# Two of eight experts of the second layer computed for every token, in the middle of the threshold search

## The chip, the cores and the metric

One core of one Trainium2 chip. The metric is the device time of one execution in microseconds (us). Three runs of the kernel before gave 168.7, 170.29 and 170.41 us.

## The reference

1024 tokens of 128 channels, in float32, go through two layers, each a conditioning step and a mixture of eight experts of width 512.

```python
x = x + L0_ffn(L0_cond(x, cond_8, ...), ...)     # each token takes its 2 best experts
x = x + L1_ffn(L1_cond(x, cond_8, ...), ...)     # each expert takes its 256 best tokens

# L1_ffn, the part that the change is about (n = 1024, k = 256, e = 8)
S = sigmoid(xt @ Wg).T                  # 8 x 1024 scores
G, I = top_k(S, k)                      # per expert: its 256 tokens and their scores
ex = xt[I]
hid = gelu(einsum('ekh,ehf->ekf', ex, W1) + b1[:, None, :])
out = (einsum('ekf,efh->ekh', hid, W2) + b2[:, None, :]) * G[..., None]
new_x = zeros_like(xt).at[I.reshape(-1)].add(out.reshape(-1, h))
```

## The kernel before

Each engine's program is written out by hand in one block, in the order in which the engine runs it; semaphores tie the engines together. TensorE keeps its order strictly: what stands behind a waiting instruction waits too. Tokens lie in eight chunks of 128 (`NC`), and `P` is 128.

The first layer ends with `x1`, which from there on is the running sum for the output. The second layer's conditioning (`turn_x1`, `up_gate`, `down1`, `turn_d`) gives each chunk's result twice: transposed in `dT` (channels on the partitions, all 1024 tokens side by side), and by token in `row`, which together with the scores goes to DRAM as `rows1`.

Then each expert's 256th highest score is searched (L1050 to L1075). VectorE compares all 1024 scores of an expert with 16 candidate thresholds at once (L1060), decides which hold at least 256 tokens (L1061), and TensorE adds those decisions up with one small matmul (L624 for the first digit, L628 for the five others), which gives the next digit of `tau`. After six digits TensorE spreads `tau` (L631), VectorE marks the tokens above and at it, TensorE counts the marks ahead of each token (L489 to L642), and VectorE turns the counts into slots, `hlf1h` and `loc1` (L1091 to L1099). ScalarE and GpSimd each make one half of `hlfv` from them (L825, L431).

Per expert, `place` on VectorE (L1103) and `find_slots` on TensorE (L649, eight small matmuls) give the list of tokens, `index` (L875) stores it as integers, and GpSimd issues two indirect gathers of 128 rows each (L420). `turn_xg` transposes the rows (L658), ScalarE copies them into `xgT` (L833, `take_xg`), `up1` makes 256 of the 512 hidden columns (L669, in halves h = 0 and 1), ScalarE applies the gelu (L842, two instructions for each half), and `down_e` makes the results (L679) for 128 tokens at a time. VectorE adds the bias (L1123) and multiplies with the score (L1125), `score`.

How the results get back to the tokens differs. Experts 0 to 5: GpSimd scatters them into a zeroed DRAM plane of the expert (`add`, L427, two instructions), SyncE loads the plane back (L322) once both have landed (`added`), and VectorE adds the plane to the running sum, 128x1024 at a time (`take_part`, L1132). Experts 6 and 7: VectorE builds a one-hot matrix from the token list (`spread_rows`, L1116), and TensorE multiplies the results with it, which spreads them over all tokens (`spread_out`, L689); VectorE adds that from PSUM (L1153).

GpSimd's queue is: gathers of experts 0 to 4, then for each expert its two scatters and the gathers of the expert five ahead. ScalarE's order in the expert loop is `take_xg(e + 1)`, then the gelus of expert e; TensorE's is `turn_xg(e + 1)`, `up1(e, 0)`, `down_e(e - 1)`, `up1(e, 1)`. `keep_warm` (L450) are matmuls on ones whose result nobody reads.

## Time and profile before

| | |
|---|---|
| median of three runs | 170.29 us (168.7 to 170.41) |
| profiled execution, its own time | 169.11 us |
| its span, first to last instruction | 167.3 us |
| mean granted TensorE clock | 0.939 |
| PE busy | 141.0 us (84%) |
| PE weight loads (PEld) busy | 117.8 us (70%) |
| DVE (VectorE) busy | 92.5 us (55%) |
| ACT (ScalarE) busy | 72.8 us (44%) |
| POOL (GpSimd) busy | 64.4 us (38%) |

The profiled execution's time is its span and 1.8 us around it. Busy shares are averages over stages of very different kinds; the conditioning of layer two ends at about 96 us, the threshold search at about 108 us, and the experts' matmuls at 163.65 us. A granted clock of 1.00 is TensorE at 2.4 GHz, of 0.50 at 1.2 GHz.

### The profile page before, as it was taken

Reading aid. Unit: us, or ns where it says so; the run is one execution under the profiler, and the core shown is the slowest. Engines: PE = TensorE matmul, PEld = TensorE weight load, DVE = VectorE, ACT = ScalarE, POOL = GpSimd, SP = SyncE. Lnnn points to the kernel's source line nnn. Section 1 sums busy time; section 2 is a strip of 40 time slices with the busy share of each in tenths; the row PEclk is TensorE's granted clock in tenths of the full one; section 3 lists DMA queues with packets and bytes.
Section 4 is the critical chain, followed back from the end, with each engine's and each line's share of the span. In section 5 each row is a group of like instructions: output and inputs, shape, how many; then the busy total and the mean of one; then the engine's idle time right before and its main releaser. Section 6 shows DMA issues by size and latency. Waiting matters only on the chain.

```text
span 167.3 us, 3393 instructions
## 1 busy us (share of the span) xinstructions
PE 141.0 (84%) x1044; PEld 117.8 (70%) x1044; DVE 92.5 (55%) x302; ACT 72.8 (44%) x223; POOL 64.4 (38%) x67
## 2 busy tenths in 40 slices
PE   7998959999999999994999720188889988899991
PEld 3756439999988999743999610045479877788990
DVE  0489391565553554415767988764353368436182
ACT  1678325777765656301478540000145444434100
POOL 0000376544476445624000000015777777776000
PEclk9999996999999999999699995559999999999999
DMA  5999827998898921127069240000122345515804
GB/s 163 355 427 345 254 67 218 325 297 277 281 299 246 313 108 47 35 64 220 0 264 402 92 133 0 0 2 21 50 50 66 93 135 173 174 52 157 233 17 125
DMA packets 20419, 27.52 MB, mean 164 GB/s; under 512 B 2034, under 2 KB 14706, under 8 KB 20146
## 3 DMA queue, kind: packets, MB, share of 16 engines
q1 hardware_dynamic: 17410, 22.78, 41.2%
q0 software_dynamic: 1920, 4.00, 8.0%
q10 hardware_dynamic: 1072, 0.52, 1.1%
q8 instruction: 9, 0.15, 0.4%
q14 instruction: 8, 0.07, 0.1%
HBM read 20.71 MB, written 6.59 MB: 163 GB/s over the span
## 4 chain that ended last, share of the span: by engine, by line
PE 55%; DMA 14%; DVE 12%; POOL 9%; issue 6%; ACT 1%; DVEq 0%; ACTq 0%; POOLq 0%
PE bank L538 10%; PE bank L548 9%; PE bank L679 6%; PE bank L580 5%; PE bank L689 4%; PE bank L669 4%; DMA xs<-rows,gidx 4%; DVE bsc L1060 4%; DMA xg<-rows,idx 4%; POOL xg L420 3%; DMA rows<-c_tok 2%; POOL plane L427 2%; PE bank L450 2%; DMA got<-picked 2%; PE bank L589 2%
## 5 line engine op out<-in xcount | busy, mean ns | idle before, releaser
L763 ACT ACTIVATE hT<-bank,w_now 128x128 f32<-128x128 f32 x92 | 26.2, 368 | 13.6 <-PE bank L538 13.6
L394 POOL DMA_INDIRECT xs<-rows,gidx x16 | 15.5, 969 | 27.7 <-DMA rows<-c_tok 18.8
L538 PE MATMUL bank<-xg,w_now 128*128 (+1 forms) x184 | 25.5, 283 | 0.0
L548 PE MATMUL bank<-w_sb,hT 128*128 (+1 forms) x184 | 25.1, 281 | 0.3 <-ACT hT L763 0.3
L548 PEld LDWEIGHTS bank<-w_sb,hT 128*128 128x128 f32 x184 | 23.2, 198 | 0.5 <-ACT hT L763 0.5
L538 PEld LDWEIGHTS bank<-xg,w_now 128*128 128x128 f32 x184 | 23.2, 198 | 0.5 <-issue 0.5
L450 PE MATMUL bank<-ones 128*128 128x512 bf16 x81 | 22.0, 418 | 1.1 <-DVE ones L877 1.1
L842 ACT ACTIVATE h1T<-bank,c_sb 128x256 f32<-128x256 f32 x32 | 13.4, 470 | 19.0 <-PE bank L669 19.0
L399 POOL DMA_INDIRECT picked<-y,sidx x16 | 15.4, 962 | 13.3 <-DVE y L982 12.1
L420 POOL DMA_INDIRECT xg<-rows,idx x16 | 16.9, 1058 | 6.3 <-issue 4.0
L669 PE MATMUL bank<-xgT,v_sb 128*128 128x256 f32 x64 | 16.5, 383 | 0.5 <-ACT xgT L833 0.5
L976 DVE TENSOR_TENSOR yt<-bank,b_sb 128x128 f32<-128x128 f32 x23 | 6.7, 291 | 18.0 <-PE bank L548 15.8
L679 PEld LDWEIGHTS bank<-v_sb,h1T 128*128 128x128 f32 x128 | 15.3, 192 | 1.0 <-ACT h1T L842 0.8
L679 PE MATMUL bank<-v_sb,h1T 128*128 128x128 f32 x128 | 15.9, 277 | 0.1
L427 POOL DMA_INDIRECT plane<-x_sb,idx x12 | 13.6, 1136 | 3.7 <-issue 2.7
L450 PEld LDWEIGHTS bank<-ones 128*128 128x128 bf16 x81 | 8.2, 109 | 9.4 <-issue 2.2
L431 POOL TENSOR_TENSOR hlfv<-hlf1h,cst 128x128 bf16<-128x128 bf16 x1 | 0.8, 776 | 34.5 <-DVE hlf1h L1099 34.5
L1123 DVE TENSOR_TENSOR yb<-bank,c2b_sb 128x128 f32<-128x128 f32 x16 | 4.7, 291 | 15.4 <-issue 9.3
L669 PEld LDWEIGHTS bank<-xgT,v_sb 128*128 128x128 f32 x64 | 11.0, 191 | 1.6 <-ACT xgT L833 0.7
L951 DVE COPY w_now<-w_sb 128x516 f32 (+1 forms) x23 | 11.0, 477 | 1.5 <-issue 1.5
L982 DVE SCALAR_TENSOR_TENSOR y<-yt,pairm,y 128x128 f32 (+1 forms) x23 | 8.1, 351 | 5.6 <-DVE yt L976 5.5
L580 PE MATMUL bank<-x1T,cw_sb 128*128 128x128 f32 x64 | 9.6, 298 | 0.0
(183 smaller groups left out, 208.0 us busy)
## 6 DMA issues: line engine op xcount, KB each, us to landing
v_sb<-in_v SPq DMA_DIRECT2D x16, 256.0 KB
cw_sb<-in_cond_w SPq DMA_DIRECT2D x8, 386.5 KB
plane<-y SPq DMA_DIRECT2D x6, 512.0 KB, 4.7
w_sb<-plane SPq DMA_DIRECT2D x6, 512.0 KB, 4.2
w_sb<-in_w SPq DMA_DIRECT2D x1, 2064.0 KB, 9.1
w_sb<-in_w SPq DMA_DIRECT2D x1, 1536.0 KB, 12.3
rows<-row SPq DMA_DIRECT2D x1, 544.0 KB, 3.4
xT_sb<-in_xT SPq DMA_DIRECT2D x1, 512.0 KB, 3.8
```

Source lines behind the costliest of these rows:

```text
L394: pool.indirect_dma_start(out=xs[:, b % RING], out_offset=None, in_=rows0, in_offset=rows_at(gidx, b)).then_inc(gathered[b % RING], 16)
L399: pool.indirect_dma_start(out=picked, out_offset=rows_at(sidx, b), in_=y0[:, b], in_offset=None).then_inc(scattered, 16)
L420: pool.indirect_dma_start(out=xg[:, i], out_offset=None, in_=rows1, in_offset=rows_at(idx1, i)).then_inc(gathered1[e], 16)
L427: pool.indirect_dma_start(out=plane[e], out_offset=rows_at(idx1, i), in_=y1[:, e % Y1_RING, h], in_offset=None).then_inc(added[e], 16)
L450: pe.matmul(out_bank[:], ones[:], ones[:].unsqueeze(1).to_broadcast([P, 4, P]), start=True, stop=True)
L538: mm = pe.matmul(bank[2 + j % 2][:, P * f:P * f + P], w1_now[:, j % WB_RING, P * f:P * f + P], xsT[:, bass.ds((j - e) * P, P)], start=True ...
L548: mm = pe.matmul(bank[6 + j % 2][:, 0:C], hT[:, j % 2, P * f:P * f + P], w2_sb[:, bass.ds(e * (NF * C) + f * C, C)], start=(f == 0), stop= ...
L580: mm = pe.matmul(bank[2 + b % 2][:, P * m:P * m + P], cw_sb[:, b, P * m:P * m + P], x1T[:, b % 2], start=True, stop=True)
L669: mm = pe.matmul(bank[2 + u % 3][:, CAP * f:CAP * f + CAP], v1_sb[:, e, P * fc:P * fc + P], xgT[:, e % 2], start=True, stop=True)
L679: mm = pe.matmul(bank[6 + h][:, 0:C], h1T[:, e % 2, f, P * h:P * h + P], v2_sb[:, e, f], start=(f == 0), stop=(f == NF - 1))
L763: ins = act.activation(hT[:, j % 2, P * f:P * f + P], bank[2 + j % 2][:, P * f:P * f + P], ACT.Relu, bias=w1_now[:, j % WB_RING, F + f:F + ...
L842: act.activation(h1T[:, e % 2, fc], bank[2 + (2 * e + h) % 3][:, CAP * f:CAP * f + CAP], ACT.Gelu, bias=c1_sb[:, e * NF + fc:e * NF + fc + ...
```

## The change

Experts 6 and 7 are no longer routed. They are computed for all 1024 tokens, straight from `dT`, as eight units of 256 tokens; a unit has the same matmuls and gelus as a routed expert. Six of these units (expert 6 whole and half of expert 7) stand in TensorE's order between the steps of the threshold search, the counts and the `find_slots`; the two others come at the very end. The count's PSUM moves to banks 0 and 1, the up projections use four banks (`UP_BANKS`), and the down projections two, then three (`y_bank`).

ScalarE copies the results of the six early units out of PSUM (`take_yd`), after the table load for the gelu. VectorE weights them with `wd`, which is the score where the token is among the expert's 256 and 0 elsewhere, and adds them to the running sum (`take_dense`: a bias add over up to 128x1024, then one multiply-add of 128x128 for each chunk). The results of the last two units are added straight from the bias add (`add_dense`).

`spread_rows`, `spread_out`, L1153 and GpSimd's iota go, as do two of the eight `find_slots`, `index` and gather pairs, and all `keep_warm` in this part. The six routed experts run as units 6 to 11. In ScalarE's new order `take_xg(e)` stands behind both gelus of the unit before it. VectorE makes the half of `hlfv` that ScalarE made. The plane of expert 5 is added before the last unit's results.

The diff, cut to its core:

```diff
-PLANES = 6
+SPARSE = 6
+DENSE = E - SPARSE
...
+        yd = w2_sb[:, 2 * T:4 * T].rearrange("p (e c d) -> p e c d", e=DENSE, c=NC)
+        wd = sb("wd", [P, NC, DENSE])
...
+        CHUNKS = T // CAP
+        HEAD = 6
+        UNITS = DENSE * CHUNKS + SPARSE
+        unit = [(True, SPARSE + d // CHUNKS, d % CHUNKS) for d in range(DENSE * CHUNKS)]
+        unit[HEAD:HEAD] = [(False, e, 0) for e in range(SPARSE)]
+        TAIL = range(HEAD + SPARSE, UNITS)
+        UP_BANKS = (4, 5, 2, 3)
+
+        def y_bank(n, h):
+            return 6 + n % 2 if n < HEAD else (6, 7, 1)[(NH * (n - HEAD) + h) % 3]
...
-            pool.iota(iota_t, [[1, T]], base=0, channel_multiplier=0,
-                      allow_small_or_imprecise_dtypes=True).then_inc(iota_ready, 1)
...
-                if e + GATHERS_AHEAD < E:
+                if e + GATHERS_AHEAD < SPARSE:
...
+            def count_experts(s):
                 pe.wait_ge(enough_ready, s + 1)
-                pe.matmul(bank[4][:, 0:1], same[:], enough[:], start=True, stop=True).then_inc(counted, 1)
-
-            pe.wait_ge(tau_ready, 1)
-            pe.transpose(bank[5][:, 0:P], tau[:].to_broadcast([P, P]), ident).then_inc(tau_spread, 1)
-
-
-            pe.wait_ge(gteq_ready, 1)
-            running_counts(bank[2][:, 0:NC * E], gteq[:, 0], E)
-
-            for d in range(NC):
-                pe.matmul(bank[3][:, 0:NC * E], ones[:], gteq[:, 0, d * E:(d + 1) * E].unsqueeze(1).to_broadcast([P, NC, E]),
-                          start=(d == 0), stop=False)
-            for d in range(1, NC):
-                pe.matmul(bank[3][:, d * E:NC * E], ones[:], gteq[:, 1, 0:(NC - d) * E], start=False, stop=False)
-            pe.matmul(bank[3][:, 0:NC * E], tri[:], gteq[:, 1], start=False, stop=True).then_inc(prefix1, 1)
+                if s == 0:
+                    for i in range(2):
+                        mm = pe.matmul(bank[1][:, 0:1], same[:], coarse_enough[:, i:i + 1], start=(i == 0), stop=(i == 1))
+                else:
+                    mm = pe.matmul(bank[1][:, 0:1], same[:], enough[:], start=True, stop=True)
+                mm.then_inc(counted, 1)
...
+            def up1(n, h):
+                dense, e, q = unit[n]
+                rows_in = dT[:, CAP * q:CAP * q + CAP] if dense else xgT[:, e % 2]
+                if not dense:
+                    pe.wait_ge(xgT_ready, e + 1)
+                u = 2 * n + h
+                if u in (2, 3):
+                    pe.wait_ge(sc_ready, u - 1)
+                if u >= 4:
+                    pe.wait_ge(h1T_ready, 2 * (u - 4) + 2)
                 for f in range(2):
                     fc = 2 * h + f
-                    mm = pe.matmul(bank[2 + u % 3][:, CAP * f:CAP * f + CAP], v1_sb[:, e, P * fc:P * fc + P],
-                                   xgT[:, e % 2], start=True, stop=True)
+                    mm = pe.matmul(bank[UP_BANKS[u % 4]][:, CAP * f:CAP * f + CAP], v1_sb[:, e, P * fc:P * fc + P],
+                                   rows_in, start=True, stop=True)
                 mm.then_inc(h1_ready, 1)
 
-            def down_e(e):
-                pe.wait_ge(h1T_ready, 4 * (e + 1))
+            def down_e(n, h):
+                dense, e, q = unit[n]
+                pe.wait_ge(h1T_ready, 4 * (n + 1))
+                if n == 0:
+                    pe.wait_ge(row_ready, NC)
+                if 2 <= n < HEAD:
+                    pe.wait_ge(yd_kept, n - 1)
+                if n == HEAD:
+                    pe.wait_ge(yd_kept, HEAD)
+                    pe.wait_ge(idx1_ready, SPARSE)
+                if NH * (n - HEAD) + h >= 3:
+                    pe.wait_ge(y1_ready, NH * (n - HEAD) + h - 2)
+                for f in range(NF):
+                    mm = pe.matmul(bank[y_bank(n, h)][:, C * h:C * h + C], h1T[:, n % 2, f, P * h:P * h + P],
+                                   v2_sb[:, e, f], start=(f == 0), stop=(f == NF - 1))
+                mm.then_inc(y1_sent, 1)
+
+            pe.wait_ge(in_v, 16 * 2 * E)
...
+            up1(0, 0)
+            turn_scores(0)
+            count_experts(0)
+            up1(0, 1)
+            turn_scores(1)
+            count_experts(1)
+            up1(1, 0)
+            down_e(0, 0)
+            down_e(0, 1)
+            count_experts(2)
+            up1(1, 1)
+            up1(2, 0)
+            down_e(1, 0)
+            count_experts(3)
+            down_e(1, 1)
+            up1(2, 1)
+            up1(3, 0)
+            count_experts(4)
+            down_e(2, 0)
+            down_e(2, 1)
+            up1(3, 1)
+            count_experts(5)
+            up1(4, 0)
+            spread_tau()
+            down_e(3, 0)
+            count_ahead()
+            down_e(3, 1)
+            up1(4, 1)
+            up1(5, 0)
+            find_slots(0)
+            down_e(4, 0)
+            find_slots(1)
+            down_e(4, 1)
+            find_slots(2)
+            up1(5, 1)
+            find_slots(3)
+            down_e(5, 0)
+            find_slots(4)
+            down_e(5, 1)
+            find_slots(5)
+            turn_xg(0)
+            up1(HEAD, 0)
+            turn_xg(1)
+            up1(HEAD, 1)
+            for n in range(HEAD + 1, UNITS):
+                e = n - HEAD
+                if e + 1 < SPARSE:
+                    turn_xg(e + 1)
+                up1(n, 0)
                 for h in range(NH):
+                    down_e(n - 1, h)
+                up1(n, 1)
+            for h in range(NH):
+                down_e(UNITS - 1, h)
...
-            act.wait_ge(hlf1h_ready, 1)
-            act.activation(hlfv[:, :, :, 0].rearrange("p c e h -> p (c e) h"), hlf1h[:], ACT.Identity,
-                           scale=const("pcol")).then_inc(hlfv_ready[0], 1)
...
+            def take_yd(n):
+                _, e, q = unit[n]
+                act.wait_ge(y1_sent, NH * n + NH)
+                act.activation(yd[:, e - SPARSE, NH * q:NH * q + NH], bank[6 + n % 2][:, 0:NH * C], ACT.Copy).then_inc(yd_kept, 1)
+
+            for n in range(UNITS):
+                gelu(n, 0)
+                if 1 <= n <= HEAD:
+                    take_yd(n - 1)
+                e = n - HEAD + 1
+                gelu(n, 1)
+                if 0 <= e < SPARSE:
+                    take_xg(e)
...
+            v.wait_ge(hlf1h_ready, 1)
+            v.tensor_scalar(hlfv[:, :, :, 0].rearrange("p c e h -> p (c e) h"), hlf1h[:], const("pcol"), None,
+                            ALU.mult).then_inc(hlfv_ready[0], 1)
...
+            def add_dense(d, c, src):
+                return v.scalar_tensor_tensor(x1[:, c], src, wd[:, c, d:d + 1], x1[:, c], ALU.mult, ALU.add)
+
+            def take_dense(d, chunks):
+                c0, c1_ = NH * chunks[0], NH * chunks[-1] + NH
+                v.wait_ge(yd_kept, CHUNKS * d + chunks[-1] + 1)
+                now = yd[:, d, c0:c1_]
+                link(v.tensor_tensor(now, now, bc(c2b_sb[:, SPARSE + d], 1, c1_ - c0), ALU.add))
+                for c in range(c0, c1_):
+                    ins = add_dense(d, c, yd[:, d, c])
+                link(ins)
+
...
+            link(v.scalar_tensor_tensor(wd[:], posi[:].rearrange("p (c e) -> p c e", e=E)[:, :, SPARSE:E], float(CAP),
+                                        sc[:, :, SPARSE:E], ALU.is_lt, ALU.mult))
+            for d in range(HEAD // CHUNKS):
+                take_dense(d, range(CHUNKS))
+            if HEAD % CHUNKS:
+                take_dense(HEAD // CHUNKS, range(HEAD % CHUNKS))
+            for e in range(SPARSE):
                 for h in range(NH):
                     score(e, h)
-                if e == 0:
-                    index(E - 1)
-                if e == 2:
-                    spread_rows()
                 if e >= 3:
                     take_part(e - 3)
-            for e in range(E - 3, PLANES):
+            for e in range(SPARSE - 3, SPARSE - 1):
                 take_part(e)
-            for g in range(2):
-                v.wait_ge(summed, g + 1)
-                v.tensor_tensor(acc[:, 512 * g:512 * g + 512], acc[:, 512 * g:512 * g + 512], bank[(1, 5)[g]][:],
-                                ALU.add).then_inc(out_ready, 1)
+            for n in TAIL:
+                _, e, q = unit[n]
+                if n == TAIL[-1]:
+                    v.wait_ge(part_in[SPARSE - 1], 16)
+                    for g in range(2):
+                        ins = v.tensor_tensor(acc[:, 512 * g:512 * g + 512], acc[:, 512 * g:512 * g + 512],
+                                              part[SPARSE - 1][:, 512 * g:512 * g + 512], ALU.add)
+                        if g == 0:
+                            ins.then_inc(out_ready, 1)
+                        else:
+                            link(ins)
+                for h in range(NH):
+                    with_bias(n, h)
+                    ins = add_dense(e - SPARSE, NH * q + h, yb[:, n % 2, h])
+                if n < TAIL[-1]:
+                    link(ins)
+            ins.then_inc(out_ready, 1)
```

## Rows read from the trace of the kernel before

**Rows 1.** Windows: stretch; length, busy PE, PEld, DVE, ACT, POOL; granted clock; DMA share, GB/s

```profile
96.00:109.34 13.34, 2.33 (x15) 1.25 (x13) 10.52 (x42) 2.15 (x7) 0.00 (x0) 0.64 0.14 42
```

**Rows 2.** Chain that ended last, two turns of the search: start, length, what

```profile
101.67 0.20 PE bank L628
...
103.75 0.20 PE bank L628
```

**Rows 3.** Timeline of PE and ACT as conditioning ends: start, length, engine, line

```profile
95.62 1.12 PE L618 MATMUL bank<-cst,got 128*128 128x128 f32 x8
...
97.08 1.28 ACT L823 ACT_TABLE_LOAD   x1
```

**Rows 4.** Chain that ended last, from the counts to the first gathers

```profile
109.34 0.23 PE bank L489
...
110.43 0.09 PE bank L642
...
112.33 0.79 POOL hlfv L431
...
114.83 1.02 POOL xg L420
...
116.16 2.91 DMA xg<-rows,idx
...
121.15 0.43 PE bank L649 x8
```

**Rows 5.** Timeline, first routed expert and a later gather issue

```profile
119.58 0.38 ACT L833 ACTIVATE xgT<-bank 128x256 f32<-128x256 f32 x1 [6.90 <-PE bank L658]
...
121.19 0.84 ACT L842 ACTIVATE h1T<-bank,c_sb 128x256 f32<-128x256 f32 x2 [1.22 <-PE bank L669]
...
121.56 0.94 POOL L420 DMA_INDIRECT xg<-rows,idx  x1 [0.30 <-issue]
```

**Rows 6.** Chain that ended last, pieces of the expert loop and its end

```profile
127.36 0.22 PE bank L658 x2
...
147.95 1.78 PE bank L679 x16
149.74 0.88 PE bank L669 x4
...
154.51 3.57 PE bank L689 x32
...
163.67 0.69 DVE c_tok L1153
```

**Rows 7.** Timeline of VectorE and GpSimd, scatters and a plane's addition

```profile
139.84 0.99 POOL L427 DMA_INDIRECT plane<-x_sb,idx  x1 [0.30 <-issue]
...
150.10 0.29 DVE L1125 TENSOR_SCALAR x_sb<-yb,xg 128x128 f32<-128x128 f32 x1
...
150.30 1.22 DVE L1132 TENSOR_TENSOR c_tok<-c_tok,w_sb 128x1024 f32<-128x1024 f32 x1
150.38 1.97 POOL L427 DMA_INDIRECT plane<-x_sb,idx  x1 [0.31 <-DVE x_sb L1125]
```

**Rows 8.** Loads of the planes, by tile: one stretch's instruction and its landing

```profile
L322 SPq DMA_DIRECT2D w_sb<-plane x1: 360/360/360, 142.1 to 142.1; - x1
...
DMA to landing us min/median/max: 4.1/4.1/4.1
```

**Rows 9.** Loads of the planes, the last two together

```profile
L322 SPq DMA_DIRECT2D w_sb<-plane x2: 360/360/360, 153.4 to 154.9; - x2
...
DMA to landing us min/median/max: 4.0/4.8/5.5
```

**Rows 10.** Line L399, layer one's scatters: ns min/median/max, first and last start

```profile
L399 POOL DMA_INDIRECT picked<-y,sidx x16: 957/957/983, 43.5 to 71.4; - x16
```

**Rows 11.** Windows as in Rows 1, around a fall and a rise of the clock

```profile
79.50:80.00 0.50, 0.50 (x4) 0.50 (x4) 0.10 (x1) 0.26 (x1) 0.00 (x0) 0.50 0.00 0
...
82.50:83.00 0.50, 0.50 (x5) 0.50 (x5) 0.50 (x3) 0.48 (x2) 0.00 (x0) 0.76 0.00 0
```

More of the change, by code:

```diff
@@ L694, in _ @@
-            pe.wait_ge(in_v, 16 * 2 * E)
-            keep_warm(bank[7], 6)
-            for hlfv_part in hlfv_ready:
-                pe.wait_ge(hlfv_part, 1)
-            for e in range(AHEAD):
-                find_slots(e)
-                keep_warm(bank[7], 3)
-            turn_xg(0)
-            up1(0, 0)
-            find_slots(AHEAD)
-            up1(0, 1)
-            find_slots(AHEAD + 1)
-            turn_xg(1)
-            find_slots(AHEAD + 2)
-            down_e(0)
-            up1(1, 0)
```

144 lines of the change are left out of this document (50 added, 94 removed).

## The prediction

> **What bounds the kernel now.** I read the granted clock first, then the chain of waits, then the timeline from 95 us to the end, engine by engine. During the threshold search VectorE alone is busy: between 96 and 109.34 us it works 10.5 of 13.3 us and TensorE 2.3, at a mean clock of 0.64 [rows 1]. One digit takes 2.08 us from one counting matmul to the next [rows 2]. That idle time is what the change wants to fill. Behind the search the chain goes over counts, slots and the first gather [rows 4], and from about 120 us to 163.65 us TensorE is the bound almost without a break, the last pieces being the spreads of experts 6 and 7 [rows 6]. The planes of experts 0 to 5 come back beside that. The last load starts at 154.9 and lands between 158.9 and 160.4 us (4.0 or 5.5 later [rows 9]), which VectorE can still take before the last spread. I therefore ask of the change how late the experts' phase starts, how fast TensorE gets through it, and what then comes last.
>
> **TensorE's work.** A half of `up1` costs 0.87 us and the two halves of `down_e` 1.78 [rows 6], so a unit is 2 x 0.87 + 1.78 = 3.52 us. Before there are eight units (28.2 us) and 64 spread matmuls in two pieces, 7.6 us (the first piece shows 3.57 for 32 records [rows 6], and there are 64 of them). After there are 14 units, 49.3 us, of which six (21.1) lie in the head. In the experts' phase eight units stay, as before, and the spreads go. If nothing else stood in the way, that would be the gain: 7.6 us less what the head takes longer.
>
> **The head.** I take 95.6 us, where TensorE begins the score transposes now [rows 3], and add what it must do up to the end of `up1(6, 1)`: six units 21.1, the two halves of unit 6 1.7, transposes 1.1 [rows 3], six digit matmuls of 0.20 [rows 2] 1.2, the spread of `tau` 0.3 (an estimate; it is one transpose), counts 1.1 (109.34 to 110.52 [rows 4], at 1.2 GHz; at 2.4 GHz down to 0.6), six `find_slots` between 0.43 [rows 4] and 0.65, taken at 0.5, 3.0, and two transposes of gathered rows with the first copy 1.0 [rows 5, 6]. That is 30.5 us. To it come gaps. The first two digit decisions come from VectorE as before, and TensorE stands some 0.5 us before each. The larger gap is a new wait: `down_e(0, 0)` needs four gelus, and ScalarE must first copy the scores (0.4), load its table (1.28 [rows 3]) and do two pairs of 0.84 [rows 5]. With the second transposes done at 99.0 that is 102.5 us, while TensorE has finished `up1(1, 0)` at 100.6: 1.9 us of waiting, and `count_experts(2)` is queued behind it, so the search stands still too. With 0.3 for switching, `up1(6, 1)` ends at 95.6 + 30.5 + 1.0 + 1.9 + 0.3 = 129.3 us.
>
> In the search itself each digit leaves TensorE about 1.9 us before the next decision, and the list puts 2.6 to 3.5 us of unit work between them (three or four halves). The count is late each time, and VectorE waits. Following the list item by item, the third count falls at 104.3 instead of 101.67 [rows 2], `tau` is spread near 113.7, the counts end at 115.8 instead of 110.5, `hlfv` is there at about 118.4 (2.6 us for the slots and `hlfv` as now, 110.52 to 113.12 [rows 4]), and the first gather starts at 120.1 instead of 114.83 [rows 4]. It lands 4.2 us later (two issues and 2.91 [rows 4]), before TensorE wants it at 126.6. The delay of the search by 5 us is thus covered by unit work; the cover is thin only where units are done and slots are not. The `hlfv` half that moves from ScalarE to VectorE, and `wd`, are single small instructions of about 0.25 us each (estimate; every small VectorE instruction here takes 0.15 to 0.3): at most 0.3 us on the path, inside the rounding. The iota and the cleared `keep_warm` cost nothing and free nothing that anyone waits for.
>
> **The routed phase has a new stall.** Before, ScalarE copied `xgT` of the next expert ahead of both gelus of this one. Now `take_xg(e)` stands behind `gelu(n, 1)`, and that gelu needs `up1(n, 1)`, the last item of the turn. TensorE's next item, `turn_xg(e + 1)`, overwrites the PSUM that this copy reads, and waits for it. Whatever was gathered early, TensorE stands each turn for two gelus (0.84), a copy (0.38) and two handovers of 0.04 [rows 5]: 1.27 us. This happens ahead of `turn_xg(2)` to `turn_xg(5)` and once more ahead of `up1(11, 0)`, five times, 6.3 us. Nothing in the trace of before shows this wait, as the order was another; its bounds are 0 (were the copy free to go first) and 1.3 us each, and I take the upper one, because every part has its row and the order admits no other. The five turns are 4 x (1.27 + 0.27 + 3.52) + (1.27 + 3.52) = 25.0 us, and the first half of the sixth, `up1(12, 0)` and `down_e(11)`, 2.65. `down_e(11, 1)` ends at 129.3 + 25.0 + 2.7 = 157.0 us.
>
> VectorE and GpSimd keep up with this. `take_dense` is one bias add of 1.22 (as L1132 [rows 7]) and eight multiply-adds, about 4 us, and for the two chunks of expert 7 another 2; it ends near 133 us and makes the first `score` 1.6 us late. GpSimd then scatters expert 0 and gathers expert 5 by 139, landing by 143.5 at the latest (behind a plane load of 4.1 to 5.5 us [rows 8, 9]). TensorE wants it at 145.8, thanks to the stalls.
>
> **The end.** Between `down_e(11, 1)` and TensorE's last matmul lie three halves of `up1` and two pairs of `down_e`, 6.2 us: until 163.2. That is no later than 163.65 now, so TensorE's end, two VectorE steps (1.0) and the 2.94 us from VectorE's last instruction to the end of the span (163.67 + 0.69 to 167.3 [rows 6]) would give 167.1. But the plane of expert 5 now has only these 6.2 us to come back. The result is scored 0.65 us after its matmul (149.74 to 150.39 [rows 6, 7]), at 157.65. The second scatter starts 0.6 us later, behind the first (0.99 and 0.3 each [rows 5, 7]), and as `take_part(2)` has just started on VectorE it loses about 0.55 more: a scatter that started 0.08 us into a plane's addition took 1.97 instead of 0.99 [rows 7]. From an undisturbed start to the plane's arrival it is 6.4 us (139.84 to 142.1 and 4.1 [rows 7, 8]), at most 7.8 (5.5 in place of 4.1 [rows 8, 9]); I take the first, since no second load runs beside it. The plane is in at 157.65 + 0.6 + 0.55 + 6.4 = 165.2. Then come two additions of 128x512 (1.3, half of 1.22 each and a handover [rows 7]), two bias adds and two multiply-adds of 128x128 (four of some 0.33, 1.35), and 2.94 to the end. 165.2 + 1.3 + 1.35 + 2.94 = 170.8 us of span, against 167.3: 3.5 us more, 2.1%. The profiled execution's time lies 1.8 us above its span, which makes 172.6 against 169.1. The median of the runs before is 1.2 us above that execution; on it I forecast 170.3 + 3.5 = 173.8 us.
>
> **A rule that speaks against this.** The scatters in layer one, which run beside VectorE's multiply-adds with both inputs in SBUF (L982), take 0.957 to 0.983 us [rows 10], so those short instructions hold nothing up; only the 1.22 us addition does. The Trainium skill, GPSIMD Engine Reference, section "Key points", says that GpSimd shares its SBUF interfaces with VectorE and contends with instructions that have two SBUF inputs. By that rule taken strictly all of `take_dense` would hold up the gathers, which is what rival 3 prices; the trace agrees for the long form only.
>
> **Rivals.** (1) A clock fall in the head. After the pause between the layers the clock was at 0.50 by 79.5 us and rose between 82.5 and 83.0 [rows 11], so some 3.3 us at 1.2 GHz. The 0.5 and 1.9 us gaps could bring that on, and TensorE, now the bound of the head, would lose half of it: +1.7, 175.5 us. Against it speaks that work resumes at once. (2) The plane is not last. If its way back, from score to landing, took 3.7 us less than the 7.5 that I reckon, TensorE's end would decide: 167.1 of span, 170.1 us, no change. No load in the rows is that fast. (3) Gathers held up by `take_dense`: 6 us of it instead of 1, expert 5 lands at 147 instead of 143.5, TensorE waits 1.5 us: 175.3. (4) The other side: no stall for `xgT`, because ScalarE's copy gets done in time. The point is whether `take_xg` ends before `up1(n, 1)` does. Then 6.3 us go, the gather of expert 5 becomes the wait (2 us), the chain over the plane stays: span 166.5, 169.5 us. Were the plane hidden as well, it would be span 162.8 (without the gather's wait 160.8), 165.8 us: faster. Whether the digits come somewhat earlier or later changes none of this, as unit work fills the head either way.
>
> **How the numbers follow.** Forecast 173.8, chance 0.40. Rival 1 0.20, rival 3 0.08, rival 2 0.15, rival 4 with the plane last 0.09, with both wrong 0.08. About 1% is what a measurement of this kernel can tell from no change, that is 168.6 to 172.0 us. Faster is the last case, 0.08. Same are rival 2, rival 4's first form and the lower edge of the forecast (the head 1.5 us shorter), 0.27. Slower is the rest, 0.65. The range goes from 169.3, just under the cases of no change, to 176.3 us, the clock's case with 0.8 for the bounds of the plane's way and the counts.
>
> **What the profile would show.** Right: a granted clock near 1.00 in place of 0.64 during the search; digits 2.5 to 4 us apart; one TensorE gap near 101 us for L842's gelu; the first `find_slots` about 5 us later; then five gaps of 1.3 us ahead of the transposes, released by ScalarE's copy; and at the end VectorE waiting for a DMA, some 2 to 4 us after TensorE's last matmul. Wrong, if those five gaps are missing or are released by gathers, if the last plane arrives before TensorE ends, or if the clock falls to 0.50 between 100 and 130 us.

## The result and the profile after

The changed kernel takes 176.19 us (median of four runs, 175.26 to 177.23) against 169.5 us for the kernel before (four runs, 168.63 to 170.41). The medians lie 6.7 us apart (4.0%). The ratio on record is 1.0465 with a 95% interval of 1.0419 to 1.0512, which would be some 7.8 us; the eight times do not account for the difference, and this text goes by the medians and the trace. Slower it is by either. The forecast was slower by 3.5 us (2.1%). Medians here are of all executions, while ratios leave out those more than 1.5% above the same kernel's fastest. The profiled execution took 175.26 us, its span 173.3 us.

The page of the changed kernel first: busy time by engine, and TensorE's granted clock in 40 slices of 4.3 us.

```profile
PE 147.7 (85%) x1086; PEld 125.3 (72%) x1086; DVE 92.3 (53%) x308; ACT 83.5 (48%) x250; POOL 58.2 (34%) x62
...
PEclk9999999999999999999999969999999999999998
```

The clock stands near full speed through the search, where it was 0.64 [rows 1]; one slice, from 99.6 us, shows a 6. The timeline of TensorE, by its own waits, through the threshold search (start, length, instruction, and in brackets the idle time before it and what ended it):

```profile
95.31 0.20 PE L633 MATMUL bank<-coarse_enough,same 128*128 128x1 bf16 x2 [0.40 <-DVE coarse_enough L1088]
...
97.42 0.18 PE L635 MATMUL bank<-enough,same 128*128 128x1 bf16 x1 [0.50 <-DVE enough L1093]
...
100.27 3.65 PE L703 MATMUL bank<-v_sb,h1T 128*128 128x128 f32 x16 [1.70 <-ACT h1T L873]
...
103.75 0.17 PE L635 MATMUL bank<-enough,same 128*128 128x1 bf16 x1
...
109.55 0.17 PE L635 MATMUL bank<-enough,same 128*128 128x1 bf16 x1
...
112.59 0.17 PE L635 MATMUL bank<-enough,same 128*128 128x1 bf16 x1
...
124.12 1.16 PE L703 MATMUL bank<-v_sb,h1T 128*128 128x128 f32 x8 [0.45 <-ACT h1T L873]
```

The first two digits are 2.1 us apart, as before [rows 2]. Then TensorE stands 1.70 us ahead of `down_e(0, 0)`, with the third count queued behind it (6.3 us to the next digit), and from there the digits are 2.7 to 3.1 us apart, because unit work lies in front of each. The `down_e(0)` that follows takes 3.65 us for 16 matmuls, where the same pair behind the same pause takes 2.05 in the runs below whose clock stays up: the clock has fallen. In the pause itself (98.60 to 100.20 us) it was still granted at 1.00. The windows around it (length, busy PE, PEld, DVE, ACT, POOL, then the granted clock), and those of the two stages:

```profile
95.30:130.20 34.90, 31.35 (x236) 26.99 (x236) 18.80 (x62) 14.80 (x37) 8.34 (x9) 0.95 0.10 29
130.20:159.30 29.10, 22.29 (x150) 19.52 (x150) 11.27 (x33) 11.55 (x30) 15.36 (x15) 1.00 0.37 110
...
101.00:102.00 1.00, 1.00 (x7) 1.00 (x6) 0.00 (x0) 0.00 (x0) 0.00 (x0) 0.50 0.00 0
103.00:104.00 1.00, 1.00 (x7) 0.99 (x7) 0.00 (x0) 0.04 (x1) 0.00 (x0) 0.68 0.00 0
```

In the head TensorE works 31.35 of 34.9 us; in the routed rounds only 22.29 of 29.1. Where most of those 6.8 us go is seen at the transposes of the gathered rows, again on TensorE's timeline:

```profile
131.56 0.41 PE L671 MATMUL bank<-cst,xg 128*128 128x128 f32 x2 [1.35 <-ACT xgT L864]
...
136.84 0.41 PE L671 MATMUL bank<-cst,xg 128*128 128x128 f32 x2 [1.35 <-ACT xgT L864]
...
142.12 0.41 PE L671 MATMUL bank<-cst,xg 128*128 128x128 f32 x2 [1.35 <-ACT xgT L864]
...
147.40 0.41 PE L671 MATMUL bank<-cst,xg 128*128 128x128 f32 x2 [1.36 <-ACT xgT L864]
...
152.59 1.13 PE L686 MATMUL bank<-xgT,v_sb 128*128 128x256 f32 x4 [1.26 <-ACT xgT L864]
```

Five gaps, each released by ScalarE's copy (line 864, which was line 833), 5.28 us from one turn to the next. The end of the span, from the chain of waits:

```profile
159.54 0.96 POOL plane L434
...
160.81 3.12 DMA plane<-x_sb,idx
...
163.94 3.92 DMA w_sb<-plane
...
167.95 0.10 DVE c_tok L1201
...
170.19 0.35 DVE c_tok L1167
```

The last result of expert 5 is scattered, its plane is loaded, and only then can VectorE finish. TensorE has ended at about 167.2 us (163.65 before); the load lands at 167.86.

To compare kernels I use the **stage** from the first digit matmul (line 624 before, 633 after) to the end of the span. What lies ahead of it is nearly the same work in every kernel here and still ended between 95.3 and 100.3 us in the traces of the chips without the unexplained waits shown further below. Before it is 97.47 to 167.3, 69.8 us; after it is 95.31 to 173.3, 78.0 us, of which 1.6 us is the clock (3.65 against the 2.05 us that the same 16 matmuls take in the traces where the clock stays up), so 76.4 without. The changed kernel's digit is 2.2 us earlier in part because its clock did not fall between the layers, where the kernel before spent 3.3 us near half speed [rows 11]. So of the fall one pays about as much in either trace, and 76.4 - 69.8 = 6.6 us agrees with the medians' 6.7. A stage is read from one execution each.

### The profile page after: what moved, and what is told of

It reads as the page before. It is cut to its first block, busy times and chain, and to the rows that moved or that the text cites. A ratio compares the mean times of both kernels' runs of the same rounds, so it can differ in the third digit from the quotient of the medians.

```text
span 173.3 us, 3525 instructions
## 1 busy us (share of the span) xinstructions
PE 147.7 (85%) x1086; PEld 125.3 (72%) x1086; DVE 92.3 (53%) x308; ACT 83.5 (48%) x250; POOL 58.2 (34%) x62
## 4 chain that ended last, share of the span: by engine, by line
PE 59%; DMA 14%; ACT 8%; DVE 8%; issue 5%; POOL 3%; ACTq 0%; DVEq 0%; POOLq 0%
PE bank L703 13%; PE bank L545 10%; PE bank L686 9%; PE bank L555 9%; ACT h1T L873 5%; DMA xs<-rows,gidx 4%; PE bank L587 3%; DMA w_sb<-plane 2%; PE bank L457 2%; DMA got<-picked 2%; DMA rows<-c_tok 2%; DMA plane<-x_sb,idx 2%; POOL picked L408 2%; PE bank L662 2%; PE bank L596 1%
## 5 line engine op out<-in xcount | busy, mean ns | idle before, releaser
L873 ACT ACTIVATE h1T<-bank,c_sb 128x256 f32<-128x256 f32 x56 | 23.3, 472 | 25.8 <-PE bank L686 25.5
L703 PE MATMUL bank<-v_sb,h1T 128*128 128x128 f32 x224 | 30.6, 290 | 3.6 <-ACT h1T L873 3.1
L703 PEld LDWEIGHTS bank<-v_sb,h1T 128*128 128x128 f32 x224 | 28.5, 202 | 6.5 <-ACT h1T L873 6.2
L403 POOL DMA_INDIRECT xs<-rows,gidx x16 | 15.7, 980 | 26.2 <-DMA rows<-c_tok 17.9
L434 POOL DMA_INDIRECT plane<-x_sb,idx x12 | 12.7, 1055 | 13.1 <-DVE x_sb L1157 10.9
L457 PE MATMUL bank<-ones 128*128 128x512 bf16 x63 | 16.1, 406 | 1.1 <-DVE ones L909 1.1
L686 PE MATMUL bank<-w_eff,v_sb 128*128 128x256 f32 x64 | 16.1, 386 | 0.0
L427 POOL DMA_INDIRECT xg<-rows,idx x12 | 12.9, 1074 | 5.7 <-issue 3.0
L686 PE MATMUL bank<-xgT,v_sb 128*128 128x256 f32 x48 | 12.6, 384 | 1.7 <-ACT xgT L864 1.7
L686 PEld LDWEIGHTS bank<-w_eff,v_sb 128*128 128x128 f32 x64 | 11.4, 191 | 1.2
L457 PEld LDWEIGHTS bank<-ones 128*128 128x128 bf16 x63 | 6.5, 106 | 7.9 <-issue 1.1
```

The costliest lines, as they stand in the source:

```text
L403: pool.indirect_dma_start(out=xs[:, b % RING], out_offset=None, in_=rows0, in_offset=rows_at(gidx, b)).then_inc(gathered[b % RING], 16)
L427: pool.indirect_dma_start(out=xg[:, i], out_offset=None, in_=rows1, in_offset=rows_at(idx1, i)).then_inc(gathered1[e], 16)
L434: pool.indirect_dma_start(out=plane[e], out_offset=rows_at(idx1, i), in_=y1[:, e % Y1_RING, h], in_offset=None).then_inc(added[e], 16)
L457: pe.matmul(out_bank[:], ones[:], ones[:].unsqueeze(1).to_broadcast([P, 4, P]), start=True, stop=True)
L686: mm = pe.matmul(bank[UP_BANKS[u % 4]][:, CAP * f:CAP * f + CAP], v1_sb[:, e, P * fc:P * fc + P], rows_in, start=True, stop=True)
L703: mm = pe.matmul(bank[y_bank(n, h)][:, C * h:C * h + C], h1T[:, n % 2, f, P * h:P * h + P], v2_sb[:, e, f], start=(f == 0), stop=(f == NF ...
```

## The experiments

Four questions: does the place of `take_xg` make the five gaps; does the pause ahead of `down_e(0, 0)` bring the clock down; is the plane last at the end; and is the late search really covered by unit work?

**The copy ahead of the gelu.** In ScalarE's loop:

```
                 e = n - HEAD + 1
+                if 1 <= e < SPARSE:
+                    take_xg(e)
                 gelu(n, 1)
-                if 0 <= e < SPARSE:
+                if e == 0:
                     take_xg(e)
```

> The changed kernel, with one line of ScalarE's order moved: take_xg(e) stands between the two gelus of a unit instead of behind both (for experts 1 to 5). Theory A (the order makes the five pauses of 1.35 to 1.7 us ahead of the transposes of gathered rows): the pauses go or shrink below 0.3 us, save one wait of up to 2 us for the gather of expert 5; the rounds fall from 5.28 us towards 3.9 us and the time falls by 4 to 6.5 us against the changed kernel, to 170 to 172 us. Rival B (the rounds are paced by GpSimd's queue and the planes, and the copy only happens to be the releaser): the pauses stay, released by a DMA, and the time falls by less than 2 us.

Measured: 171.17 us, 1.0149 of before (1.0036 to 1.0261; before 168.91 on that chip), so it is 2.3 us slower than the kernel before beside it where the change was 6.7: some 4.4 us of the 6.7 are gone (5.3 by the two ratios). The stage is 72.1 us, 4.3 less than 76.4. Its timeline of TensorE at the same transposes:

```profile
130.32 0.41 PE L671 MATMUL bank<-cst,xg 128*128 128x128 f32 x2 [0.54 <-ACT xgT L864]
134.09 0.38 PE L671 MATMUL bank<-cst,xg 128*128 128x128 f32 x2
137.99 0.38 PE L671 MATMUL bank<-cst,xg 128*128 128x128 f32 x2
142.60 0.44 PE L671 MATMUL bank<-cst,xg 128*128 128x128 f32 x2 [0.54 <-DMA xg<-rows,idx]
```

and its chain of waits:

```profile
138.07 4.49 DMA xg<-rows,idx
...
153.63 0.96 POOL plane L434
...
154.90 4.29 DMA plane<-x_sb,idx
...
159.20 4.02 DMA w_sb<-plane
```

A turn takes 3.8 to 3.9 us in place of 5.28 and its gap is gone (0.54 us of the first one stay): the copy's place was the cause. Not all of the five gaps' 6.7 us came back, for two reasons that these rows show. The gather of expert 5, which the gaps had given time, is now waited for (142.60 comes 4.6 us after the turn before). And the plane's way back is longer: its scatter's data take 4.29 us where they took 3.12, so that from the end of `down_e(11)`'s first half to the end of the span it is 16.0 us (152.62 to 168.6) against 14.8 (158.53 to 173.3).

**The table load ahead of the scores.** `act.activation(scrap[:], bb_sb, ACT.Gelu)`, which loads the table of gelu, moved ahead of the loop that copies the scores:

```
+            act.activation(scrap[:], bb_sb, ACT.Gelu)
             for g in range(2):
                 act.wait_ge(s_turned, g + 1)
 ...
-            act.activation(scrap[:], bb_sb, ACT.Gelu)
```

> The changed kernel, with the gelu's table loaded ahead of the two score copies, where ScalarE waits for TensorE anyway, instead of behind them. Theory A (the pause ahead of down_e(0, 0) costs its own 1.7 us and brings a stretch at 1.2 GHz, which costs about 1.8 us more): the pause falls below 0.5 us, the clock stays at 1.00 through the search, and the time falls by 3 to 3.5 us. Rival B (the clock's fall has nothing to do with the pause): 1.2 to 1.6 us less, and the clock still falls. Rival C (the head has slack before the gathers): less than 1 us.

Measured: 174.51 us, 1.0382 (1.029 to 1.0475); stage 74.75, 1.65 less than 76.4. Its rows of the first digit, of `down_e(0)` and of the first transposes:

```profile
97.35 0.20 PE L633 MATMUL bank<-coarse_enough,same 128*128 128x1 bf16 x2 [0.39 <-DVE coarse_enough L1088]
...
100.79 2.05 PE L703 MATMUL bank<-v_sb,h1T 128*128 128x128 f32 x16 [0.18 <-ACT h1T L873]
...
126.02 0.41 PE L671 MATMUL bank<-cst,xg 128*128 128x128 f32 x2
```

The pause of 1.70 us is 0.18, and the stage is shorter by about that much. The load cost what the pause showed and nothing more. Of the expectations the size is rival B's, but the clock stays up behind the pause, as theory A had it. The last row, the first transposes of gathered rows, is used further below.

**The pause filled.** `down_e(0, 0)` still waits as long, but TensorE does idle matmuls in the meantime:

```
             up1(1, 0)
+            keep_warm(bank[7], 7)
             down_e(0, 0)
```

> The changed kernel, with seven matmuls on ones that nobody reads put into TensorE's pause ahead of down_e(0, 0); the pause itself stays, filled. Theory A (the pause is what lets the clock fall): the two halves of down_e(0) take 1.8 us instead of 3.65, and the time falls by 1.6 to 2 us. Rival B (the clock falls at some time of its own in any case): no change of the time beyond 0.8 us, and a stretch at 0.50 elsewhere in the head.

Measured: 176.69 us, 1.0437 (1.033 to 1.0543); stage 76.5. No gain, which is rival B's size. Its timeline:

```profile
101.32 1.67 PE L457 MATMUL bank<-ones 128*128 128x512 bf16 x7
103.18 2.05 PE L703 MATMUL bank<-v_sb,h1T 128*128 128x128 f32 x16 [0.19 <-ACT h1T L874]
```

The clock stays up behind the filled pause. But it also stayed up behind the unfilled one, in the run with the copy moved (101.46) and in the next one (105.21):

```profile
101.46 2.05 PE L703 MATMUL bank<-v_sb,h1T 128*128 128x128 f32 x16 [1.70 <-ACT h1T L873]
```
```profile
105.21 2.05 PE L703 MATMUL bank<-v_sb,h1T 128*128 128x128 f32 x16 [1.69 <-ACT h1T L873]
```

So a fall can follow this pause and need not, and the filled run does not show that the filling prevented one. Both of these unfilled runs had a fall between the layers (slices of 8 and 7 near 80 us), and so had the filled one (0.50 between 80 and 82 us). The run of the changed kernel had none there and one here. One later run (six early units refitted, below), in which the pause is 0.18 us, had none in either place. Why a run takes one or the other is not settled.

**Without the last plane.** This kernel leaves out the wait for the plane of expert 5 and adds the plane of expert 4 a second time in its place, so its output is not the right one; the instructions stay the same.

```
-                    v.wait_ge(part_in[SPARSE - 1], 16)
 ...
-                              part[SPARSE - 1][:, 512 * g:512 * g + 512], ALU.add)
+                              part[SPARSE - 2][:, 512 * g:512 * g + 512], ALU.add)
```

> The changed kernel without its last wait: the plane of expert 5 is not added at the end, plane 4 is added there a second time in its place, so that the instructions are the same and only the wait for the load of plane 5 goes. It shows what the plane's way back costs at the end. Theory A (the plane is last, by what the trace shows: it lands 0.6 us after TensorE's last matmul and two additions follow): the time falls by 2 to 2.7 us. Rival B (TensorE's end would set the time anyway, with the additions behind it): less than 1 us.

Measured: 174.87 us, 1.0352 (1.0249 to 1.0456); stage 74.65, 1.75 less (it begins late in this trace, at 100.25 us, which the stage's length leaves out). The chain now passes over the plane of expert 4:

```profile
160.23 2.56 DMA plane<-x_sb,idx
...
162.80 4.09 DMA w_sb<-plane
```

The last plane costs 1.75 us at the end, as much as VectorE's wait for it in the changed kernel (1.80 us ahead of line 1201) and a little less than the 2 to 2.7 us of theory A. Rival B's less than 1 us is out.

**Both edits together, and other sizes of the head.** The next kernels all take the copy and the table edit (the first has only these), and the others write TensorE's list anew so that only as much unit work stands between two digits as fits into the time VectorE takes, with 6, 5 or 4 of the eight dense units ahead of the routed ones (`HEAD`); the rest come last:

```
+up1(0, 0) turn_scores(0) count_experts(0) up1(0, 1) turn_scores(1) count_experts(1)
+up1(1, 0) down_e(0, 0) count_experts(2) down_e(0, 1) up1(1, 1) count_experts(3)
+up1(2, 0) down_e(1, 0) count_experts(4) down_e(1, 1) up1(2, 1) count_experts(5)
+spread_tau() count_ahead() up1(3, 0) down_e(2, 0) down_e(2, 1) find_slots(0)
+up1(3, 1) find_slots(1) down_e(3, 0) find_slots(2) down_e(3, 1) find_slots(3)
+up1(4, 0) find_slots(4) up1(4, 1) find_slots(5)
+down_e(4, 0) down_e(4, 1)
```

This is the list for five units. For four, only `find_slots(4)` and `find_slots(5)` stand behind `find_slots(3)`; for six, `up1(5, 0)` stands ahead of `down_e(4, 0)` and the rest of unit 5 at the end.

> Both edits of the first two experiments together: take_xg between the gelus, the gelu's table loaded early. From the first digit's matmul (L633) to the end of the span the changed kernel takes 76.4 us where its clock does not fall, the kernel before 69.8; the first edit gave 72.1, the second 74.75. Theory A (the two add up, since one shortens the head and the other the rounds): 70.6 us of this stage, and a time within 1% of the kernel before. Rival B (the plane of expert 5 or the gathers take back what the head gives): 71.5 us or more.

> As e5, still six early units, but in another order on TensorE: never more than two halves (1.8 us) between two digits, none between the last digit and the counts, three ahead of the first find_slots, and the other ten between and behind the find_slots. The digits thus keep their 2.1 us. Theory A (the prediction's: unit work fills TensorE in the head whichever way it is ordered, so late digits cost nothing): within 0.7 us of e5's stage. Rival B (the delayed digits delay slots, gathers and everything behind them): 2 us or more faster than e5.

> As e6, with five early units and three at the end. Theory A (about four units fit into TensorE's idle time in the search; each further one lengthens the head by 2 to 3.5 us and the end loses 3.5, but the plane of expert 5 then waits at the end): the three at the end, 9.8 us of TensorE behind the last routed result, just cover the plane's 7.7 us and the additions, so the stage takes 65 to 67.5 us, and the time is 1.5 to 3% below the kernel before. Rival B (gathers and GpSimd's queue pace the rounds): 69 us or more, no gain on the kernel before.

> As e6, with four early units (expert 6) and four at the end (expert 7): the early work is what fits into the search without delaying it. Theory A: the first find_slots starts 15.7 to 16.5 us behind the first digit's matmul, as in the kernel before, the plane of expert 5 is in long before TensorE ends, and the stage takes 65.5 to 68 us. Rival B (as with five): 69 us or more.

Measured: 180.24, 184.05, 182.49 and 182.03 us, on a chip on which the kernel before took 183.22 (179.86 to 184.74). No ratio came of it. The same four kernels once more, on another chip:

> The kernel of e5 again, as e5 to e8 fell on a chip where the kernel before itself took 183 us and several engines stood still for 1.4 to 6 us at a time with no releaser in the trace. Both theories as for e5: A 70.6 us from the first digit's matmul to the end of the span and a time within 1% of the kernel before; B 71.5 us or more.

> The kernel of e6 again: six early units in the order that leaves the digits alone. In e6 the first find_slots began 15.7 us behind the first digit's matmul, as in the kernel before, instead of 20.1 in e5. Theory A (what counts is how much unit work TensorE has, not where the digits stand): stage within 0.7 us of e9. Rival B (late digits cost): 2 us or more below e9.

> The kernel of e7 again: five early units in that order, three at the end. Theory A: 65 to 68 us of stage, 1.5 to 3% below the kernel before, since the three late units cover the plane of expert 5. Rival B: 69 us or more.

> The kernel of e8 again: four early units, four at the end. Theory A: 65.5 to 68.5 us of stage, within 1 us of the one with five, because what the head gains the end gives back. Rival B: 69 us or more.

Measured, before at 184.3: 184.4 (ratio 1.0175, 1.0002 to 1.0348), 185.82 (1.0258, 1.0132 to 1.0383), 183.08 (1.0067, 0.9995 to 1.0138) and 186.44 us (no ratio). The kernel before was itself 14 us above its time on the first chip, so it was profiled there too, and with it a tail in which the last unit's second `up1` half goes ahead of the `down_e` before it:

```
                 up1(n, 0)
+                if n == UNITS - 1:
+                    up1(n, 1)
                 for h in range(NH):
                     down_e(n - 1, h)
-                up1(n, 1)
+                if n < UNITS - 1:
+                    up1(n, 1)
```

> The kernel before, profiled on the same chip as the three that follow, so that stages can be set side by side on one chip. No theory differs here: 69.8 us from the first digit's matmul to the end of the span where no engine stands still without a releaser, as in its first profile; more where such pauses come.

> The kernel of e5 and e9: both ScalarE edits, six early units in the order of the change. If the two edits add up: 70.6 us of stage, 0.5 to 1% above the kernel before beside it.

> The kernel of e6 and e10: six early units, digits left alone. Theory A (late digits cost nothing as long as TensorE is full): within 1 us of e14's stage, up to 1 us more. Rival B (late digits cost): 2 us or more below e14.

> Five early units as in e7 and e11, and both up1 halves of the last unit ahead of the down_e of the unit before it, which takes the last wait for a gelu (0.9 us) out. Theory A (the plane is hidden behind three late units, TensorE is the bound): 67.7 to 69 us of stage, 0.5 to 1.5% below the kernel before beside it. Rival B (what is won in the search goes at the end or to the gathers): 70 us or more, no gain on the kernel before.

Measured, before at 182.69: the kernel before once more 185.02 (1.0039, 0.9947 to 1.0131), copy and table 185.18 (1.0164, 1.0074 to 1.0254), six units 188.25 (1.0229, 1.0141 to 1.0318), five with the tail 184.16 (no ratio). The waits of the unchanged kernel (engine, line, what it waited for, then us in total, times, longest):

```profile
DVE yt L976 <- remote: 8.0, 3, 3.3
...
ACT h1T L842 <- remote: 7.7, 1, 7.7
```

Such waits, which no instruction or transfer in the trace ends ("remote"), stand in every kernel on these three chips and in none on the others. They are longer than the differences asked for, so the expectations on the stage are not decided here. What these three sets do say is by pieces that have no such wait in them. From the third expert's transposes to the end of the span it is 38.2 to 38.6 us with six early units refitted (three traces), 39.1 with five and the plain tail, 39.0 with five and the other tail, and 43.7 with four (one trace each; a second trace each of five with the plain tail, 40.2, and of four, 43.3, has such a wait of 4.8 us on VectorE within the piece). With four early units the end is thus some 5 us longer than with six; whether the head gains as much these traces cannot show. By the ratios of the second set, five units (1.0067) are ahead of six (1.0258), with intervals that just meet.

**The same on a chip without such waits** (before 168.96, 14 runs, 167.43 to 172.35): six units refitted, and five with the tail.

> The kernel of e6, e10 and e15 once more, for a trace without pauses that have no releaser. With digits delayed, both ScalarE edits together come to 70.6 us of stage by the sum of e1 and e2. Theory A (late digits are covered): 70 to 71.6 us here. Rival B (late digits cost): 68.5 us or less. If the pauses are there again: the same pause-free pieces as before, find_slots(0) at 15.7 us and 38.2 to 38.6 us from the third transposed expert to the end.

> The kernel of e16 once more, for the same reason. Theory A (TensorE is the bound, the plane hidden): 67.7 to 69 us of stage without pauses, at most 1.5% below the kernel before. Rival B: 70 us or more. With the pauses there: no difference from the kernel before beside it that clears its interval.

Measured: 172.79 us for six (1.0243, 1.0173 to 1.0313; stage 72.7), 167.83 us for five (0.994, 0.9899 to 0.9981; stage 68.65). The timeline of TensorE with six:

```profile
97.84 0.20 PE L633 MATMUL bank<-coarse_enough,same 128*128 128x1 bf16 x2 [0.40 <-DVE coarse_enough L1090]
...
102.28 0.17 PE L635 MATMUL bank<-enough,same 128*128 128x1 bf16 x1
...
108.59 0.18 PE L635 MATMUL bank<-enough,same 128*128 128x1 bf16 x1
116.16 1.16 PE L703 MATMUL bank<-v_sb,h1T 128*128 128x128 f32 x8 [0.45 <-ACT h1T L873]
126.93 2.05 PE L703 MATMUL bank<-v_sb,h1T 128*128 128x128 f32 x16 [0.99 <-ACT h1T L873]
128.81 0.38 PE L671 MATMUL bank<-cst,xg 128*128 128x128 f32 x2
...
132.43 0.41 PE L671 MATMUL bank<-cst,xg 128*128 128x128 f32 x2 [0.55 <-ACT xgT L864]
```

Now the digits keep the 2.1 us of [rows 2], and the first `find_slots` comes 15.7 us after the first digit, as before, in place of 23.2. The time does not follow: the stage is 72.7 us, against 72.1 for the copy's edit alone and 70.5 by the sum of the copy's and the table's edit, both of which this kernel has. It lies outside both expectations (70 to 71.6, and 68.5 or less). The head shows why. With late digits and the table's edit, the first transposes of gathered rows come 28.7 us after the first digit (126.02 - 97.35, in the second experiment); with the digits on time they come after 31.0 us (128.81 - 97.84). (The first trace of both edits, on one of the chips above, has 29.5 us with late digits, 0.67 of it a wait that the others lack.) In between TensorE works 27.1 and 27.7 us, so it stands 1.5 us in the one and 3.2 in the other: it now waits for the spread of `tau` (0.25) and for the counts (0.45), and for a gelu ahead of the last `down_e` (0.99). The work that was taken from between the digits had to be done later, and the gathered rows lay ready before TensorE came to them. That settles the fourth question: with six units in the head, late digits cost nothing, and on-time digits cost 2.3 us. With five, the chain ends so:

```profile
135.20 4.49 DMA xg<-rows,idx
...
152.03 4.61 DMA plane<-x_sb,idx
...
156.66 3.88 DMA w_sb<-plane
```

The third expert's transposes come at 127.67 in place of 132.43 (30.4 us after the first digit, not 34.6), and from there to the end it is 38.2 us against 38.1, although a third unit stands there: TensorE's last matmul ends at 161.16 us, just behind the plane, which lands at 160.54. The unit taken out of the head fits beside the plane's way back. This version is well ahead of the changed kernel. The kernel before it beats by 0.6%: the interval leaves out 1, but the difference is less than the 1% that I called measurable beforehand. It differs from the six in two things, the unit and the tail. The head's 4.2 us (30.4 against 34.6) go with the unit, 3.5 us of work and part of a wait; what the tail adds was not measured alone, and on the chips above the two tails gave 39.0 and 39.1 us for the same piece. Five units with late digits were not tried.

## Why the prediction was half right

**Direction and places: right.** All five gaps stood where the prediction put them, released by ScalarE's copy, at 1.35 us against 1.27, and moving the copy took 4.3 us out of the stage. The pause ahead of `down_e(0, 0)` was there (1.70 us against 1.9). The plane of expert 5 was last: 7.7 us from score (160.13) to landing (167.86) against 7.55, and from the end of `down_e(11, 1)` to the end of the span 14.0 against 13.8. Rival 4 (the copy in time) and rival 2 (the plane not last) are out. The delay of the search was covered, as said; with the digits on time the head was 2.3 us longer. Two of the signs came out otherwise: the plane landed 0.6 us after TensorE's last matmul, not 2 to 4, and the clock did fall to 0.50 between 100 and 130 us, which the prediction had named as a sign of being wrong.

**Size: half.** Forecast +3.5 us, measured +6.7. The steps that failed are two terms of the sum, the head and the rounds: both were added up from durations of items that follow another without a wait.

*The head.* It was to end 31.8 us after the first digit (129.3 - 97.47). It took 34.9, and 33.3 without the fall of the clock: 1.5 us too little. I took each `down_e` half as half of a pair, 0.89 us. A half that stands alone between other items takes longer, as the chain of waits of the changed kernel shows:

```profile
113.84 1.06 PE bank L703 x8
...
119.14 1.00 PE bank L703 x8
```

Eight of the twelve halves stand so. They take 0.97 to 1.16 us there, the longest where they follow a wait, and together some 1.2 us more than reckoned. At 124.12 TensorE waits again for gelus (0.45 us on the matmuls); I had allowed one such wait, not two. Against these stand 0.3 us less in the gaps foreseen (0.40, 0.50 and 1.70, not 2.9). These are the largest differences and not a full account: the two whole pairs took 2.05 us each (with the clock up) and not 1.78, while the counts took 0.7 and not 1.1.

*The rounds.* They were to take 27.7 us from `up1(6, 1)` to the end of `down_e(11, 1)` and took 29.1. A turn is 5.28 us, not 5.06: 0.9 us in the four turns, of which 0.08 each is the gap and 0.14 each the transposes, which take 0.41 us behind it and not 0.27. The other 0.5 us is of the same kind: the half of `up1` behind the fifth gap took 1.13 us (152.59 above) and not 0.87, and `down_e(11)`, which follows a short wait for a gelu at 157.36, took 2.05 and not 1.78. The chain of waits of the kernel before has both durations, behind waits of its own:

```profile
120.02 1.13 PE bank L669 x4
...
151.59 2.05 PE bank L679 x16
```

The prediction took the other rows, 0.87 and 1.78 [rows 6], for every place. Behind the routed rounds the two late units wait for gelus again (0.99 us ahead of the last `down_e`), so TensorE needed 7.9 us where I had 6.2. That one was hidden: TensorE ended at 167.2, just ahead of the plane.

1.5 for the head, 1.4 for the rounds and 0.2 for the end are 3.1 us: 3.5 + 3.1 = 6.6, the stage's difference. One error lies behind most of it: the durations were those of items that follow another of long matmuls without a wait, and in the new list short items take turns and many follow a wait. That the start of an item is otherwise hidden behind the one before is my reading of these rows; no run tested it.

**Rival 1, the clock,** happened in the profiled run, at the size given (1.6 against 1.7 us), but it was no added cost: that run had no fall between the layers, and runs with the same pause had none behind it. I had priced it on top of a fall that it replaced.

**Rival 3, gathers held up by `take_dense`,** was rightly small. The timelines of GpSimd and VectorE in the changed kernel show which gathers were slower:

```profile
127.56 1.22 DVE L1173 TENSOR_TENSOR w_sb<-w_sb,c2b_sb 128x1024 f32<-128x1024 f32 x1
128.09 1.51 POOL L427 DMA_INDIRECT xg<-rows,idx  x1 [0.30 <-issue]
129.90 0.94 POOL L427 DMA_INDIRECT xg<-rows,idx  x1 [0.30 <-issue]
131.15 1.41 POOL L427 DMA_INDIRECT xg<-rows,idx  x1 [0.30 <-issue]
```

The gathers at 128.09 and 131.15 began within additions with two SBUF inputs (the one at 127.56, and one of 0.69 us at 131.05) and took 1.51 and 1.41 us; that at 129.90, beside multiply-adds of 128x128, took 0.94, and so did the one at 132.86. The Trainium skill, GPSIMD Engine Reference, section "Key points", has GpSimd contend with VectorE instructions that have two SBUF inputs, without regard to their size. The trace agrees only for issues that began within a long float32 addition: the gather at 126.84, already under way when the addition at 127.56 began, took 0.94 too. TensorE waited for none of these gathers.

## What to carry to other kernels

When work is inserted into a rotating loop, write down each engine's order across the turn, not only the new engine's: one copy placed behind the gelu in ScalarE's list cost more than any other item measured here, on an engine that was half idle. Idle time of an engine is filled only up to what fits, and the rest of the moved work is then paid for where nothing hides it; here five of eight early units, with the tail reordered, came out level with or just ahead of the kernel before and six did not, as the end had a wait of its own that a late unit could cover. Keeping the search on time was worth nothing as long as its results were not what TensorE waited for. Take the durations of short alternating items, and of items behind a wait, from a place where such items already stand so, and look for the second and third instance of any wait that the sum finds once.

## What the runs showed of the hardware

**Engines that stand still for no reason in the trace.** On three chips the unchanged kernel took 183 to 185 us in place of 169. It was profiled on one of them, where engines waited up to 7.7 us at a time with nothing in the trace that ends the wait; in the changed kernels on all three such a wait was up to 12.0 us. They keep their places: in five of the six traces taken there with six or five early units refitted, three `idx` instructions in a row wait 2.3 to 2.4, 3.5 to 3.6 and 3.5 to 3.6 us. What causes it is open.

**A gather behind a load.** The gather of expert 5, issued some 0.3 us behind the start of a plane's load, took 4.49 us to land (in two kernels), where the first gather landed after 2.91 [rows 4]. That is the wait that comes next once the five gaps are gone.

**The clock after a pause.** Behind the same pause of 1.70 us, TensorE's granted clock was 0.50 (1.2 GHz) in one run and 1.00 (2.4 GHz) in two. In the one run it was 1.00 through the pause and fell as the work resumed.

**A group of matmuls behind a wait.** In the chains of waits the same group takes longer where it follows a wait: two transposes 0.41 us against 0.22 to 0.28, a half of `up1` 1.13 against 0.87, a pair of `down_e` 2.05 against 1.78.

Open remain what chooses the place of the clock's fall, what the waits without a releaser are, and how far the copy and the table edit together, which were timed only on chips with such waits, stand from the kernel before; by the two stages they would give 78.0 - 1.6 - 4.3 - 1.65 = 70.5 us against 69.8, while the two ratios taken beside such waits put them 1.6 to 1.8% above it.
